# A graph layer with edge scatter-adds on one core: side transfers cut into steps, first eight edge columns on two tables

## What is computed

```python
xn = layernorm(x)
in_deg, out_deg = counts of dst and of src, at most 511
sum3d = segment_sum(edge_attr @ W_sum + b_sum, src)
gnn = xn + z_in[in_deg] + z_out[out_deg] + sigmoid(cent * W_cent + b_cent) + sigmoid(vor * W_vor + b_vor) + sum3d
mix = linear attention over all nodes, 8 heads, then @ w_out + b_out
x = x + gnn + mix
x = x + ffn(layernorm(x))     # 8 experts, 256 -> 1024 -> 256, the two best of each node
```

## Time and profile before

| | |
|---|---|
| three timed runs | 2674.8, 2677.9, 2684.9 us |
| profiled execution | 2665.9 us, of which the span from first to last instruction is 2664.0 |
| busy | PE 64%, VectorE 47%, ScalarE 27%, GpSimd 63% |
| scatter-adds (L1418) | 782, busy 1244.1 us, last at 1612 us |
| DMA engines | busy 90% and more up to 200 us, 80% to 400, 70% to 670, about 50% until 1530 (slices of 67 us) |
| HBM | read 247.03 MB, written 108.96 MB |

### The profile page before, as it was taken

The page is one execution under the profiler, slowest core; times in us unless marked ns, Lnnn a source line. Parts: engine busy times, 40 slices in busy tenths (PEclk is TensorE's granted clock), DMA queues, the critical chain, the costliest instruction groups (busy, mean ns, idle before and its releaser), DMA issues.

```text
span 2664.0 us, 33981 instructions
## 1 busy us (share of the span) xinstructions
PE 1711.4 (64%) x10955; PEld 1312.6 (49%) x10955; DVE 1248.1 (47%) x3231; ACT 726.1 (27%) x1605; POOL 1685.8 (63%) x1107
## 2 busy tenths in 40 slices
PE   2443445556666666666666634775877878777876
PEld 1211233334444444444554524664866767666765
DVE  2334334334444444444665542558645555545453
ACT  1011123333223222321211102443433333333332
POOL 3766777778888888888888888880233333333332
PEclk9656657777778777887888857986999989989998
DMA  9998887777555555555555547885367666666664
GB/s 274 202 164 115 142 139 125 125 110 103 71 71 68 70 71 71 71 71 71 69 69 71 71 34 138 179 159 184 98 203 220 206 205 204 207 195 214 194 215 113
DMA packets 373460, 358.28 MB, mean 134 GB/s; under 512 B 43317, under 2 KB 340738, under 8 KB 358692
## 3 DMA queue, kind: packets, MB, share of 16 engines
q0 software_dynamic: 146880, 92.09, 33.1%
q1 hardware_dynamic: 226404, 264.03, 32.8%
HBM read 247.03 MB, written 108.96 MB: 134 GB/s over the span
## 4 chain that ended last, share of the span: by engine, by line
DMA 52%; POOL 21%; issue 13%; PE 9%; DVE 2%; SPq 1%; POOLq 1%; ACT 0%; DVEq 0%; ACTq 0%
DMA node_table<-edge_sums,row_i 30%; POOL node_table L1418 19%; DMA result<-mixw,slot_tok 12%; DMA state<-L_gnn_z_in,in_deg 6%; PE bank L678 4%; DMA edge_rows<-xn_rows,slot_tok 4%; PE bank L664 2%; POOL edge_rows L1451 1%; PE bank L632 1%; PE bank L634 1%; PE bank L650 1%; SPq L1488 1%; POOL result L1463 0%; DMA node_numbers<-id_rows 0%; POOLq L1418 0%
## 5 line engine op out<-in xcount | busy, mean ns | idle before, releaser
L1418 POOL DMA_INDIRECT node_table<-edge_sums,row_i x782 | 1244.1, 1591 | 363.8 <-DMA node_table<-edge_sums,row_i 173.8
L446 PE MATMUL bank<-edge_rows,same_node 128*128 128x130 f32 x1564 | 314.8, 353 | 578.5 <-issue 372.7
L446 PEld LDWEIGHTS bank<-edge_rows,same_node 128*128 128x128 f32 x1564 | 270.5, 251 | 729.6 <-issue 695.3
L1463 POOL DMA_INDIRECT result<-mixw,slot_tok x105 | 168.7, 1607 | 454.6 <-DMA result<-mixw,slot_tok 312.7
L1229 ACT COPY edge_sums<-bank 128x390 f32<-128x390 f32 (+1 forms) x261 | 126.4, 484 | 1199.3 <-DMA node_table<-edge_sums,row_i 1138.9
L1372 ACT ACTIVATE mixw<-bank,m_r 128x256 f32<-128x256 f32 (+1 forms) x456 | 242.5, 549 | 494.7 <-PE bank L664 333.9
L678 PE MATMUL bank<-big 128*128 128x256 f16 x2520 | 315.7, 290 | 1.0 <-issue 1.0
L664 PE MATMUL bank<-edge_rows,big 128*128 128x256 f16 (+1 forms) x2736 | 286.8, 265 | 5.4 <-DMA big<-w_parts 5.4
L678 PEld LDWEIGHTS bank<-big 128*128 128x128 f16 x2520 | 260.4, 104 | 44.4 <-issue 1.3
L664 PEld LDWEIGHTS bank<-edge_rows,big 128*128 128x128 f16 x2736 | 250.6, 98 | 34.4 <-DMA big<-w_parts 7.4
L546 PE MATMUL bank<-mixw,big 128*128 128x512 f32 x392 | 264.8, 812 | 4.0 <-ACT big L1282 4.0
(11 more groups left out here) (255 smaller groups left out, 2382.2 us busy)
## 6 DMA issues: line engine op xcount, KB each, us to landing
big<-w_parts SPq DMA_DIRECT2D x114, 1024.0 KB, 5.8
edge_rows<-edge_attr SPq DMA_DIRECT2D x130, 384.0 KB, 3.9
big<-L_ffn_W SPq DMA_DIRECT2D x128, 128.0 KB, 3.5
w_parts<-big SPq DMA_DIRECT2D x64, 256.0 KB, 3.9
node_table<-zeros SPq DMA_DIRECT2D x20, 645.0 KB, 8.7
node_table<-edge_sums,row_i POOLq DMA_INDIRECT x782, 3.6
mixw<-node_table SPq DMA_DIRECT2D x96, 129.0 KB, 3.7
b2r<-L_ffn_b SPq DMA_DIRECT2D x57, 128.0 KB
```

Source lines behind the costliest of these rows:

```text
L446: ins = e.matmul(ps_sum[:, i * XW:(i + 1) * XW], S[:, g % SRING, i * P:(i + 1) * P], X[:, c // LOAD % XRING, c % LOAD, :], start=True, sto ...
L1418: e.indirect_dma_start(table[t], bass.IndirectOffsetOnAxis(ap=row_i[:, g % ORING, i:i + 1], axis=0), O[:, g % ORING, i, 0:RW], None, compu ...
L1463: e.indirect_dma_start(y_rows, bass.IndirectOffsetOnAxis(ap=slot_tok[:, tile:tile + 1], axis=0), yo[:, j % 2, s, :], None, compute_op=ALU. ...
```

## The change

1. `table_of(c)` gives the table of a column and how many columns went there before. Columns 0 to 7 alternate between tables 0 and 1; from 8 on it is c % 4 again. The prologue zeroes table 0 whole before the numbers are stored, then table 1 whole; tables 2 and 3 follow behind the edge loads.
2. `load_weights` is issued as three, three and two pieces at stages 0, 1 and 2. The wait for the raw buffer stands before the first piece.
3. The high store's second half moves from stage 11 to stage 12, the low store's from 13 to 14, and the low store's first half waits only for the first half of the low part. There is one side step more for the weights (W_TICKS).
4. `load_x` issues one DMA a step instead of four every fourth step; the first chunk is still loaded at once.

The numbers and sizes of the DMAs are those of before.

```diff
--- before.py
+++ after.py
@@ -30,6 +30,7 @@
 LOADS = -(-ETILES // LOAD)
 XRING, SRING, ORING = 4, 3, 6
 TABLES = 4
+EARLY = 8
 XW = EDIM + 2
 RW = EDIM + 1
 ROWS = (TILES + 1) * P
@@ -60,7 +61,7 @@
 N8 = TILES * EXPERTS
 
 
-W_TICK0, W_TICKS = 2, (2 * EXPERTS - 1) * WEVERY + 14
+W_TICK0, W_TICKS = 2, (2 * EXPERTS - 1) * WEVERY + 15
 W_META = W_TICK0 + W_TICKS
 NORM_END = 1 + 4 * XCH
 MIX0, MIX_EVERY = NORM_END + 16, 3
@@ -71,6 +72,13 @@
 
 def tiles_of(g):
     return range(g * GROUP, min(ETILES, (g + 1) * GROUP))
+
+
+def table_of(c):
+
+    if c < EARLY:
+        return c % 2, c // 2
+    return c % TABLES, (c - EARLY) // TABLES + (EARLY // 2 if c % TABLES < 2 else 0)
 
 
 def side_due(tick):
@@ -405,7 +413,8 @@
 
     def table_free(e, c):
 
-        e.wait_ge(table_added[c % TABLES], 16 * (c // TABLES + 1))
+        t, before_it = table_of(c)
+        e.wait_ge(table_added[t], 16 * (before_it + 1))
 
     def all_added(e):
         for c in range(ETILES - TABLES, ETILES):
@@ -1410,11 +1419,11 @@
         if 0 <= g < GROUPS:
             e.wait_ge(edge_rowed, 2 * (g // 2) + 2)
             for i, c in enumerate(tiles_of(g)):
-                t = c % TABLES
-                if c < TABLES:
+                t, before_it = table_of(c)
+                if before_it:
+                    e.wait_ge(table_added[t], 16 * before_it)
+                else:
                     e.wait_ge(table_zero[t], 16 * PIECES)
-                else:
-                    table_free(e, c - TABLES)
                 e.indirect_dma_start(table[t], bass.IndirectOffsetOnAxis(ap=row_i[:, g % ORING, i:i + 1], axis=0),
                                      O[:, g % ORING, i, 0:RW], None, compute_op=ALU.add, bounds_check=ROWS - 1,
                                      oob_is_err=True).then_inc(table_added[t], 16)
@@ -1528,16 +1537,14 @@
         e.wait_ge(idx_dve, IDX_PADDED)
         load_numbers(e, src)
         e.wait_ge(const_dve, DVE_ZEROS)
-        zero_table(e, 0, range(3))
+        zero_table(e, 0, range(PIECES))
         store_numbers(e, 0)
-        zero_table(e, 0, range(3, PIECES))
         load_number_rows(e, 0)
         load_edges(e, 0)
-        load_edges(e, 1)
-        zero_table(e, 1, range(1))
+        zero_table(e, 1, range(PIECES))
         for c in range(1, CH):
             store_numbers(e, c)
-        zero_table(e, 1, range(1, PIECES))
+        load_edges(e, 1)
         load_edges(e, 2)
         for i in range(2, TABLES):
             zero_table(e, i, range(PIECES))
@@ -1560,16 +1567,18 @@
             e.dma_start(b1_r, b1.rearrange("e (h p) -> (e h) p", p=P)).then_inc(ln_load, 16)
         w = u - W_TICK0
         if 0 <= w < W_TICKS:
-            if (n := at_stage(w, 13, WEVERY, 2 * EXPERTS)) is not None:
-                which, ex, r = matrix(n)
-                e.wait_ge(w_low, 2 * n + 2)
-                for a in range(0, WN, WN // 2):
-                    e.dma_start(w_parts[which][ex][:, WN + a:WN + a + WN // 2], low[r][:, a:a + WN // 2]).then_inc(w_low_store[r], 16)
-            if (n := at_stage(w, 11, WEVERY, 2 * EXPERTS)) is not None:
-                which, ex, _ = matrix(n)
-                e.wait_ge(w_high, n + 1)
-                for a in range(0, WN, WN // 2):
-                    e.dma_start(w_parts[which][ex][:, a:a + WN // 2], high[n % 2][:, a:a + WN // 2]).then_inc(w_high_store[n % 2], 16)
+            for piece in range(2):
+                if (n := at_stage(w, 13 + piece, WEVERY, 2 * EXPERTS)) is not None:
+                    which, ex, r = matrix(n)
+                    e.wait_ge(w_low, 2 * n + piece + 1)
+                    part_ = slice(piece * HID, (piece + 1) * HID)
+                    e.dma_start(w_parts[which][ex][:, WN:2 * WN][:, part_], low[r][:, part_]).then_inc(w_low_store[r], 16)
+            for piece in range(2):
+                if (n := at_stage(w, 11 + piece, WEVERY, 2 * EXPERTS)) is not None:
+                    which, ex, _ = matrix(n)
+                    e.wait_ge(w_high, n + 1)
+                    part_ = slice(piece * HID, (piece + 1) * HID)
+                    e.dma_start(w_parts[which][ex][:, 0:WN][:, part_], high[n % 2][:, part_]).then_inc(w_high_store[n % 2], 16)
             if at_stage(w, 8, WEVERY, 2 * EXPERTS) == EXPERTS - 1:
                 e.wait_ge(b1_peak, 16)
                 e.dma_start(b1_all, b1_peak_rows.rearrange("p e -> (p e)").partition_broadcast(P)).then_inc(b1_peak, 16)
@@ -1584,13 +1593,14 @@
             if (n := at_stage(w, 6, WEVERY, 2 * EXPERTS)) is not None:
                 e.wait_ge(w_peak, n + 1 + min(n + 1, EXPERTS))
                 e.dma_start(peak_rows[n:n + 1, :].rearrange("o p -> p o"), peaks[:, n:n + 1]).then_inc(peak_store[n % 2], 16)
-            if (n := at_stage(w, 0, WEVERY, 2 * EXPERTS)) is not None:
-                load_weights(e, n)
+            for stage, pieces in enumerate((range(0, 3), range(3, 6), range(6, 8))):
+                if (n := at_stage(w, stage, WEVERY, 2 * EXPERTS)) is not None:
+                    load_weights(e, n, pieces)
         if u == W_META:
             e.wait_ge(meta_dve, 9)
             e.dma_start(meta.rearrange("e p n -> p e n"), b1_t).then_inc(meta_store, 16)
 
-    def load_weights(e, n):
+    def load_weights(e, n, pieces):
         which, ex, r = matrix(n)
         src_ = w2[ex].rearrange("(h p) n -> p h n", p=P) if which else w1[ex].rearrange("(k p) n -> p k n", p=P)
         to = raw[r].rearrange("p (h n) -> p h n", h=HC if which else KC)
@@ -1598,21 +1608,22 @@
             cuts = [(slice(a, a + 1), slice(0, DIM)) for a in range(HC)]
         else:
             cuts = [(slice(k, k + 1), slice(a, a + DIM)) for k in range(KC) for a in range(0, HID, DIM)]
-        if n == 0:
+        if n == 0 and pieces[0] == 0:
             e.wait_ge(idx_dve, IDX_DST)
             e.wait_ge(id_first, 16)
             e.wait_ge(id_rest, 16 * (CH - 1))
-        if n >= RAW:
+        if n >= RAW and pieces[0] == 0:
             e.wait_ge(w_low_store[r], 32 * (n // RAW))
-        for a, b in cuts:
+        for a, b in cuts[pieces[0]:pieces[-1] + 1]:
             e.dma_start(to[:, a, b], src_[:, a, b]).then_inc(w_load[r], 16)
 
-    def load_x(e, i):
-        lo, hi = i * XPER, min((i + 1) * XPER, TILES - 1)
-        for a in range(lo, hi, 2):
-            b = min(a + 2, hi)
+    def load_x(e, i, s):
+        hi = min((i + 1) * XPER, TILES - 1)
+        a = i * XPER + 2 * s
+        b = min(a + 2, hi)
+        if a < hi:
             e.dma_start(state[:, a:b, :], x[a * P:b * P, :].rearrange("(t p) n -> p t n", p=P)).then_inc(x_load[i], 16)
-        if i == XCH - 1:
+        if i == XCH - 1 and s == 3:
             e.wait_ge(edge_const, EDGE_ZEROS)
             e.dma_start(state[0:LAST, TILES - 1, :], x[(TILES - 1) * P:NODES, :]).then_inc(x_load[i], 16)
 
@@ -1640,11 +1651,12 @@
 
     def sync_mix(e, u):
         if u == 0:
-            load_x(e, 0)
+            for s in range(4):
+                load_x(e, 0, s)
         if 1 <= u < NORM_END:
             i, s = divmod(u - 1, 4)
-            if s == 0 and i + 1 < XCH:
-                load_x(e, i + 1)
+            if i + 1 < XCH:
+                load_x(e, i + 1, s)
             if s == 3:
                 load_small(e, i)
```

## The result

The changed kernel is slower: 2703.5 us (median of four runs, 2694.3 to 2712.8) against 2676.4 us before, ratio 1.0103, 95% interval 1.0070 to 1.0136. In a later series against more runs of before the ratio was 1.0072 (1.0048 to 1.0096). The forecast was 2681, with 2656 to 2702. So the loss is small, 1.0% and 0.7%, but clear of noise in both series: 19 to 27 us where +3 was forecast. The time lies 1.5 us above the range.

The account below looks back on a forecast made before the run. Bound by 782 scatters queued on POOL, where only stalls, mostly at 4-byte peak stores, can change. Early columns +0.5, bursts -2.5, behind and ahead of peak stores +6, behind the peak wait -1: +3, timed 2681 us, range 2656 to 2702.

Parts of the forecast that it names:

- What bounds the kernel: First 1612 us: 782 scatters queued on POOL; only 140 us of stalls can change, 78 of them at 4-byte peak stores.
- The term behind the peak wait: After SP's wait for the peak store, 512 KB still goes out; follow-on stall stays or shrinks: -1 us (-4 to +4).
- The price of what stands behind: 640 KB more right behind each peak store lengthens its stall; 0.5 us per 384 KB makes +0.8 a period.
- Rival A: Slower: SP's data right behind the peak store lengthens the 4-byte windows; +18 us, 2696 us, chance 0.20.
- What stands ahead: 256 KB less ahead of each peak store's 4-byte writes is worth between 0 and -1.35 us a period.
- Rival B: Faster: data ahead of the peak store counts, data behind does not; -25 us with bursts, 2653 us, chance 0.17.
- Bursts: Until 201 us: x one transfer a step and weights over three steps take away burst stalls; -2.5 us (0 to -5).
- The early columns: First 60 us: late number rows cut the gain to 0.8 us, fuller queues cost some; +0.5 us (-0.8 to +3).
- The cover: 60 to 700 us: 15 to 20 us of ready scatters before POOL hide longer waits of DVE and PE, costed at nothing.
- Rival D: Slower: late weight pieces eat the ready scatters and POOL waits for rows; +64 us, 2742 us, chance 0.05.
- Rival C: SP catches up and pieces leave in bunches as before, so the change does nothing; 0, 2678 us, chance 0.15.
- The signs: Six scatters before 45 us, 16 stalls of 4 to 6 us, counts within two of 65 and 190.

Follow-up runs that it names:

- second profile: The changed kernel run and profiled once more, no further edit; ratio 1.0072 (1.0048 to 1.0096) to the kernel before, +19 us.
- stores_only: The kernel before with only the high and low stores issued one piece a step; ratio 1.0014 (0.9991 to 1.0038), +4 us.
- split_pe: The kernel before with x, weights and stores in pieces, peaks spread by PE instead of 4-byte stores, no early columns; ratio 0.9731, 2590.7 us.
- early8_rows: The kernel before with eight early columns and the second load of number rows ahead of zeroing tables 2 and 3; ratio 0.9990, -3 us.
- early16_rows: The kernel before with sixteen early columns and the second load of number rows ahead of zeroing tables 2 and 3; ratio 1.0031, +8 us.
- before_pe: The kernel before without the 16 stores of 4-byte peak columns and their loads, peaks spread by PE; ratio 0.9756, -65 us.

## Why the prediction failed, point by point

By parts, the +3 was 5 for weights and stores, 0.5 for the early columns and -2.5 for x. Measured alone they were 14, 6 and 2, 22 together. The largest share of the difference, 9 of 19 us, is in the first, and there the step that failed is plain: pieces put behind the peak store were priced by the main stall alone.

- **What bounds the kernel** held: a queue of scatters on POOL, of which only stalls can move, and the stalls between 60 and 620 us hang on the 4-byte peak stores. It is the best supported reading here: their removal gave 65 us of the 78 counted.
- **The term behind the peak wait was wrong in sign.** I put -1 on it (bounds -4 and +4), since the bytes issued right after the landing are the same 512 KB. The stall that follows the landing grew instead, from 16 to 41 us over the 16 periods (32 in the second profile), where the bounds allowed +4. My explanation is that those bytes now meet a backlog: the bounds were for one step's traffic, when what counts is all that is queued by then. The kernels with one part each do not bear it out by size, as said under the table, so it is argued and not shown.
- **The price of what stands behind, +6, was sought in the main stall**, from the difference of 0.5 us between periods with and without an edge load. The main stall did not grow (72 and 70). In the changed kernel's profiles the cost lies after it, where my count ended 3 us past the landing. Both terms together were +5; the weight and store parts together measured +14 (+9 to +20). Rival A's +18 is nearer, but that is luck: its mechanism, longer 4-byte windows, did not come. Main is 4.4 us a period, 4.5 before, and only two of the sixteen stalls are over 6 us.
- **What stands ahead** may count as bounded: with 256 KB less ahead, the landing fell by 1.5 us (stores_only), where -1.35 was the bound, though medians of 9.2 to 10.1 us without any such edit make the 1.5 uncertain. Rival B was wrong that behind is free.
- **Bursts: -2.5 forecast**, x alone measured +2 with an interval that holds -4 and +8. Nothing was gained that can be seen, but the interval does not exclude the forecast either.
- **The early columns: +0.5 forecast, +6 measured** (0 to +12). The limit I named was right: number rows, which landed at 56.9 us, and POOL waited 9.46 us for the rows. But both costs came out at their bounds instead of in the middle: column 6 went at 60.4 us, not 58.4, and column 9 was 3.3 us late. Still, that 3 us is less than 6, and the runs do not tell where the rest lies, or whether it is there, given the interval.
- **The cover held.** DVE waited for late weight pieces (7.3 us in four times), and between 100 and 700 us POOL never waited for rows for more than 0.3 us at a time. Rival D did not occur. Rival C did not either.
- **The range** was missed by 1.5 us, and that much is chance: with the second series' +19 the time would lie inside it. The +14 of weights and stores is inside the +18 let into it. What has no room there is +6 for the early columns, whose upper bound was +3, and +2 for x, whose bound was 0, though both intervals reach back to these bounds. The forecast of +3 is what both series contradict.
- **The signs** that I named for being right failed too: six scatters before 45 us (the sixth went at 49.4), and counts within two of 65 and 190 (they were 62 and 182; 65 and 185 in the second profile).

What stays open: whether 1 MB of unsplit weights behind the peak store (+7 us) costs less than 640 KB of pieces, two of them behind the wait (+10), for the intervals overlap; how the loss divides between the part in flight and the backlog after it; and the early columns' +6.

By the rule of the turns between the queues (the Trainium skill, "DMA: Bandwidth & Descriptors", section "Queues, rings and completion order"), a scatter should not mind SP's backlog. Without the 4-byte stores the times agree (2590.7 us in pieces, 2595.5 in bursts, not told apart). The landings agree only in part: in split_pe a scatter's median is 4.9 us from 60 to 200 us and 3.9 from 200 to 620, against 3.4 from 700 to 1500, and among the zeroing DMAs of the first 60 us it is 8.1 in early8_rows. With the 4-byte stores it is 12.0 in the window of the earlier trace rows, and what I drew from the rule does not hold.

## What to carry to other kernels

Before smoothing transfers, find the transfer that each stall ends with: here it was half a kilobyte in 128 pieces of 4 bytes, and removing the 16 such stores gave 65 us. A piece that is moved a step later is moved past everything that is issued between, so look at what it lands behind, and count the time until the queue is level again, not only the stall itself. To feed an engine earlier, its inputs, its targets and the number of targets in flight must all be there; with two of four tables a scatter can go every half landing time at best, and in early16_rows columns 8 to 12 went 2.9 to 4.3 us apart.

## What the runs showed of the hardware

A store of 128 values of 4 bytes, one from each partition, into one row of HBM takes 7.1 to 12.1 us to land in this kernel's traffic. In the two windows shown, the core's DMA falls to 62 GB/s (before) and 33 GB/s (after) meanwhile, and scatters on POOL's queue take 12 us to land instead of 3.6. Spreading the same numbers by a product on PE removed the stalls at no cost that the times show: in before_pe 72 and 221 scatters stand where 65 and 190 stood.
